# One more wait before each indirect gather of expert results, in a two-layer decoder on one core

## The reference

```python
x = x + _L0_attn_ref(_layernorm(x), ...)
x = x + _L0_xattn_ref(_layernorm(x), ctx_1024, ...)
x = x + _L0_ffn_ref(_layernorm(x), L0_ffn_Wg, L0_ffn_W1, L0_ffn_W2, L0_ffn_W3)
x = x + _L1_attn_ref(_layernorm(x), ...)
x = x + _L1_xattn_ref(_layernorm(x), ctx_1024, ctx_1024, ...)
x = x + _L1_ffn_ref(_layernorm(x), ...)
```

```python
def _L0_ffn_ref(x, Wg, W1, W2, W3):
    TOP_K = 2
    xt = x.reshape(B * S, D)
    scores = xt @ Wg.T
    topk_scores, topk_idx = jax.lax.top_k(scores, TOP_K)
    gate = jax.nn.silu(jnp.einsum('td,ehd->teh', xt, W1))
    up = jnp.einsum('td,ehd->teh', xt, W2)
    y = jnp.einsum('teh,edh->ted', gate * up, W3)
    onehot = jax.nn.one_hot(topk_idx, E, dtype=x.dtype)
    w = jnp.einsum('tke,tk->te', onehot, topk_scores)
    out = jnp.einsum('te,ted->td', w, y)
    return out.reshape(B, S, D)
```

## Time and profile before

| what | us |
|---|---|
| median of 3 runs (3332.88 to 3337.89) | 3333.81 |
| profiled execution, its time | 3340.52 |
| its span, first to last instruction | 3338.7 |
| copies of L1417: first of 135 to last | 1437.80 to 1853.37 |
| PE busy in the span | 2920.9 (87%) |
| gathers of L1337: 128, busy on POOL | 123.4 |

### The profile page before, as it was taken

The page is one execution under the profiler, slowest core; times in us unless marked ns, Lnnn a source line. Parts: engine busy times, 40 slices in busy tenths (PEclk is TensorE's granted clock), DMA queues, the critical chain, the costliest instruction groups (busy, mean ns, idle before and its releaser), DMA issues. The chain is left out here.

```text
span 3338.7 us, 77573 instructions
## 1 busy us (share of the span) xinstructions
PE 2920.9 (87%) x25090; PEld 2418.2 (72%) x25091; DVE 2261.5 (68%) x4938; ACT 2000.9 (60%) x4307; POOL 1772.8 (53%) x3168
## 2 busy tenths in 40 slices
PE   5999999799999999577888599998589999999996
PEld 4667666688888888576777477776367777778775
DVE  4777777467776666444444499998777878787642
ACT  3565555476666666343333376666487777777762
POOL 2232231346666666614444677775475767676642
PEclk9999999799999999889898799999599999999998
DMA  4444444100000000122222100000000000000000
GB/s 132 131 134 134 134 128 127 59 2 9 13 13 13 13 13 12 45 70 64 61 61 62 47 0 0 0 0 1 1 1 5 5 8 5 8 5 8 8 4 10
DMA packets 205065, 128.66 MB, mean 39 GB/s; under 512 B 14254, under 2 KB 197524, under 8 KB 204180
## 3 DMA queue, kind: packets, MB, share of 16 engines
q1 hardware_dynamic: 196628, 108.57, 11.5%
q0 software_dynamic: 8192, 16.79, 1.8%
HBM read 34.82 MB, written 90.51 MB: 38 GB/s over the span
## 5 line engine op out<-in xcount | busy, mean ns | idle before, releaser
L1546 POOL TENSOR_TENSOR a_qk<-a_qkv 128x2048 f32<-128x2048 f32 x64 | 235.4, 3678 | 55.5 <-ACT a_qkv L1521 52.7
L1479 PE MATMUL a_ps_s<-a_qk,w_ident 128*128 128x256 f32 x1024 | 235.3, 383 | 25.4 <-POOL a_qk L1546 25.3
L1337 POOL DMA_INDIRECT f_yg<-f_rows_out,f_index x128 | 123.4, 964 | 242.8 <-issue 110.7
L960 POOL TENSOR_TENSOR x_p<-x_p,x_rz 128x1232 f32<-128x1232 f32 x64 | 144.0, 2250 | 172.4 <-DVE x_rz L1069 172.3
L1479 PEld LDWEIGHTS a_ps_s<-a_qk,w_ident 128*128 128x128 f32 x1024 | 191.1, 192 | 54.4 <-issue 21.6
L1528 ACT ACTIVATE a_r<-a_o,w_a_rows 128x128 f32<-128x128 f32 x512 | 220.9, 523 | 2.1 <-DVE a_o L1578 2.1
L199 POOL TENSOR_TENSOR a_four<-stats 128x4 f32<-128x4 f32 (+1 forms) x47 | 9.7, 205 | 383.9 <-DVE stats L529 271.6
L2196 POOL TENSOR_TENSOR x_sq<-x_e 128x1232 f32<-128x1232 f32 x64 | 143.5, 2242 | 130.2 <-DVE x_t_sq L2346 130.1
L1277 PE MATMUL f_ps_y<-f_w,f_aT 128*128 x810 | 136.1, 310 | 71.5 <-DVE f_yo L1417 51.6
L512 DVE TENSOR_REDUCE a_nmax<-a_ps_s 128x4 f32<-128x512 f32 x256 | 159.0, 684 | 41.9 <-PE a_ps_s L317 41.9
L1277 PEld LDWEIGHTS f_ps_y<-f_w,f_aT 128*128 128x128 f32 x810 | 116.4, 214 | 87.9 <-issue 82.3
(11 more groups left out here) (554 smaller groups left out, 10017.4 us busy)
## 6 DMA issues: line engine op xcount, KB each, us to landing
f_rows_in<-a_zeros SPq DMA_DIRECT2D x31, 1088.0 KB, 5.4
f_rows_out<-a_zeros SPq DMA_DIRECT2D x31, 1088.0 KB, 8.8
f_xin<-f_rows_in SPq DMA_DIRECT2D x135, 64.0 KB
f_rows_out<-f_yo SPq DMA_DIRECT2D x135, 64.0 KB
out<-x SPq DMA_DIRECT2D x16, 256.0 KB
f_raw<-in_late_f SPq DMA_DIRECT2D x2, 1408.0 KB, 5.8
w_ctx<-in_ctx SPq DMA_DIRECT2D x1, 2464.0 KB
f_rows_in<-f_xr,f_where POOLq DMA_INDIRECT x128
```

The lines of the kernel that those rows point to most:

```text
L960: nc.gpsimd.tensor_tensor(wide, wide, rz[:, :].unsqueeze(2).broadcast_to([P, HEADS, K]), ALU.mult).then_inc(p_ready, 1)
L1479: ins = nc.tensor.matmul(ps_s[u % 2][:, 0:HEADS * HEADS], c.ident[:, :], qk[:, u % 2, k, :, :], start=k == 0, stop=k == HD - 1)
L1546: nc.gpsimd.tensor_tensor(qk[:, u % 2, :, :, :], qkv[:, u, 0, :, :].unsqueeze(3).broadcast_to(full), qkv[:, u, 1, :, :].unsqueeze(2).broad ...
```

## The change

One wait is added on POOL in front of every gather. For batch m of list j and gather n it asks that `y_ready` has reached `done_by(j)` + 2m + n, at most 135. Nothing else changes, and no instruction is moved.

```diff
--- before.py
+++ after.py
@@ -1334,6 +1334,7 @@
                         pool.wait_ge(sent[k], 16 * len(range(k, done_by(i // EACH), 4)))
                 wait(pool, added, i - RING + 1)
                 for n in range(2):
+                    pool.wait_ge(y_ready, min(done_by(i // EACH) + 2 * (i % EACH) + n, ALL))
                     nc.gpsimd.indirect_dma_start(yg[:, i % RING, n, :], None, yr[:, :],
                                                  bass.IndirectOffsetOnAxis(c.f0_index[:, n, i:i + 1], 0)).then_inc(gathered[i % RING], 16)
             pool.wait_ge(added, B - EACH)
```

## The result

| kernel | median, us | runs |
|---|---|---|
| before | 3333.35 | 4 (3330.01 to 3337.89) |
| with the added wait | 3276.55 | 4 (3273.99 to 3281.3) |

The ratio is 0.983, with a 95% interval of 0.9813 to 0.9848: 57 us faster. The forecast was 3265 with a range of 3224 to 3318.

What follows compares the result with a forecast made beforehand. PE bounds the kernel, losing time to late releases behind gather bursts. The 112 steps give −67.6, the last six −3.7, the end +2.1: −69.2 from 3333.8, about 3265 us, range 3224 to 3318.

Steps and rivals of the forecast that it cites:

- Burst of four from list 2 on: POOL, lists from 2 on: scalars make POOL late, so four gathers go in a row, then one per step.
- Burst of three in lists 0 and 1: POOL, first two lists: first three waits change almost nothing; fourth to eighth gathers spread, one per step.
- The period: Eight steps of the stage: 21.1 us each in lists 2 to 13, 19.4 in lists 0 and 1.
- Eight clean steps at 2.34 = 18.7: Base of each period: steps with nothing in their way take 2.34 us, read from five mid-stage steps.
- The burst's price, 1.8: Lists 2 to 13: four gathers holding 1.45 us each delay a copy by 1.8 us; three lose 0.7.
- The slower clock, 0.6: After each burst of four, PE's lower clock costs 0.6 us, half of 1.25, with ends 0 and 1.25.
- The last six steps: Stage's last six steps: 14.0 + 2.4 = 16.4 us against 20.06, a gain of 3.7.
- The end: After the last copy: list 15's first gather starts 5.0 us after it, not 2.85; +2.1 us.
- Burst broken altogether: Rival, all steps: three or four in a row hold nobody, all steps 2.34; 3232 or 3222 us; chance 0.26.
- Longer bursts: Rival, each list: fifth gather slips in, 23.3 us per list, 3296 us; chance 0.15, shared with dear single gathers.
- Nothing changes: Rival, the long gap: not the gathers' doing, issuing them later moves only them; 3334 us; chance 0.09.
- Slower: Rival, every step on ACT and DVE: each gather holds 1.45 us even alone; +68, 3402 us; chance 0.08.

Runs made afterwards that it cites:

- e3: Kernel before plus one wait at the head of each list, so all eight gathers go in a row; 3362.88 us, ratio 1.009.
- e4: Kernel before without its 128 gathers, combines adding a buffer of zeros; 3227.08 us, ratio 0.9684.
- e5: Changed kernel with POOL's 16 small instructions of each list (2 to 14) between its gathers, not ahead; 3254.21 us, 0.9755 of the kernel before.
- e6: Changed kernel with POOL's small instructions between its gathers, each gather also asking for one copy more; 3250.99 us, 0.9743 of the kernel before.

## Why the prediction was right, and where it was off

**The bound and the cause.** The reading that late releases follow bursts of gathers was right. Moving the burst moved the gap (e3), leaving the gathers out took it away (e4), and spreading them fully did too, with every gather still there (e5, e6). How a burst makes releases late, no run shows.

**Burst of four from list 2 on.** Right to the gather, in all 12 lists: four 1.24 to 1.38 us apart, then four that are spread, with POOL late through the scalars. Burst of three in lists 0 and 1: right.

**The period.** Forecast 21.1 us, measured 22.0, which is 10.9 us over lists 2 to 13. Lists 0 and 1 took 20.5 and 20.9 in place of 19.4, another 2.6. Three terms:

- *Eight clean steps at 2.34 = 18.7* is the term that was most off. I took five steps of one stretch for all eight. Without gathers a period is 19.3, since step 0 of each turn takes 2.85. The five steps do hold a step 0 (1618.10 to 1620.58), but behind the long gap it took 2.48 us and the next 2.11, so this stretch could not show it. Without gathers the 112 steps take 270.05 and not 14 · 18.7 = 261.8; that is 8.2 of the 13.5 us by which they came out longer (305.5 against 292.0).
- *The burst's price, 1.8.* The distance is 4.68, so 2.3 over a step; the step behind it takes 2.11, so the net is 2.1. For the burst of three I had 0.7; over the same lists without gathers they lost 1.5 each. The marginal price fell out differently from 1.45 held per gather. Over the same step without gathers, three in a row lose 1.5 (3.60 against 2.12, e5's list 0), four 2.3 (4.67 against 2.34), six 5.0 (7.43 against 2.44), eight 7.0 (9.87 against 2.85). From two on that is about 1.2 per further gather, near the distance at which POOL issues them; so few sizes, each read in another kernel or place, don't make a law of it.
- *The slower clock, 0.6.* Right as a mean and wrong in kind. Seven lists of the twelve lost nothing, five (4, 6, 8, 10 and 12) lost 1.4 each in step 0 (4.3 in place of 2.85). In the step of list 3 the granted clock is 1.00 (1545.86 to 1548.72), in that of list 4 it is 0.60 (1567.38 to 1571.61), after waits of PE of 1.76 and 1.81 us. PE's first product of this step, in list 3 and in list 4:

```profile
1546.05 0.42 PE L1267 MATMUL f_ps_g<-f_w_hi,f_x_hi 128*128 x1 [0.41 <-issue]
1567.57 0.66 PE L1267 MATMUL f_ps_g<-f_w_hi,f_x_hi 128*128 x1 [0.41 <-issue]
```

**The last six steps.** 16.7 against 16.4, but by luck: two errors cancel. I put the six clean steps at 14.0, and without gathers they take 11.84. I put the loss at 2.4, and it is 4.9: in list 14 not four but five gathers stand in a row behind a lone first one, and one distance of copies is 5.98.

**The end.** +2.2 against +2.1, the first gather of list 15 at 5.05 against 5.0 after the last copy. Here too the parts are off and the sum is not: that gather starts 8.0 us after the copy before the last, not 7.3, and that copy is 2.95 ahead of the last, not 2.3.

The stage's parts sum to −55.3 us. The rest of the program is 4 us shorter in the profiled execution; I don't explain that, and it is of the size of the spread between runs.

**The rivals.** *Burst broken altogether:* no, four are enough to lose 2.3. *Longer bursts:* the fifth gather never slipped in. *Nothing changes:* no, not on the chip of this pair. By the rule of the Trainium skill's page "SBUF — State Buffer", "Who interferes with whom", that PE and ACT never wait on anyone, this would have been the outcome. The measurement decides, for something that the rule, which is about SBUF's ports, does not speak of: ACT and PE waited for releases, longer when three or more indirect gathers stood in a row, and not beside six plain DMAs. On the third chip this rival would very likely have been the truth, since the kernel before shows nothing there to win; nothing in one profile could show this. *Slower:* no, gathers that stand apart cost nothing.

## What to carry to other kernels

When the instructions that release each other all become late at once, look at what another engine issues at that moment, and see whether the gap moves with it; a list in which the burst stands elsewhere can tell before any run. On a chip that shows such gaps, indirect gathers on POOL are best spread to the pace at which their results are needed, and POOL's other small work put between them rather than ahead of them, except where POOL itself ends the stage. And a gap like this can belong to the chip one measures on: run both kernels on more than one before a change is kept for it.

## What the runs showed of the hardware

- Three or more indirect gathers of 128 rows at 1.25 us held back releases between PE, ACT and DVE, and made a step longer by 1.5 us (three) to 7.0 us (eight), on two chips. Beside two in a row a step was 0.4 us longer at most; eight that stand 1.6 to 3.0 us apart held back nothing.
- It does not depend on the bytes (16 KB and 64 KB a gather: 7.4 us both), and six plain DMAs of 64 KB in a row do not do it.
- A third chip did not show it: 3236 us for the kernel that takes 3334 to 3338 on the others, and no gap beside seven gathers in a row.
- Behind the burst of four PE waited 1.8 us in most lists (1.1 in list 2, 2.2 in list 6). The granted clock of the step of the loop's turn that follows is 0.60 to 0.77 in lists 4, 6, 8, 10 and 12 and 1.00 in the seven others, at the same program.
- The first step of each turn of the hardware loop took about 2.85 us and not 2.34, with PE idle for 0.41, without gathers and behind short gaps (19.3 us a period and not 18.7); behind the long gaps of the kernel before it took 2.5.
